# The queries' softmax denominators: one sum on VectorE in place of a tree of additions on GpSimd, and a new order on four engines

## The chip, the cores and the metric

One core of one Trainium2 chip runs the whole program in one launch. The metric is the device time of an execution in microseconds (us). The kernel before took 640.22, 637.19 and 633.03 us in three executions, a median of 637.19 us.

## What is computed

Two blocks follow each other on x, 8 sequences of 1024 tokens and 256 channels, all in fp32. The first is linear attention with 16 heads of 16 channels; the second is a feed-forward layer with ternary weights. This is the first one, cut from the reference; the change touches the softmax of q:

```python
q = x @ Wq.T + bq
k = x @ Wk.T + bk
v = x @ Wv.T + bv
q, k, v = (split(q), split(k), split(v))      # (batch, heads, tokens, 16)
q = softmax(q, axis=-1)                       # over the 16 channels of a head
k = softmax(k, axis=-2)                       # over the 1024 tokens
state = einsum('bhnd,bhne->bhde', k, v)
out = einsum('bhnd,bhde->bhne', q, state)
out = layernorm(out) * ln_g + ln_b
x = layernorm(x + out @ Wo.T + bo)            # x1, the input of the feed-forward half
```

## The kernel before

**The halves.** `attention_phase` computes x1 and stores it in a scratch tensor in DRAM; then all engines meet, and `feed_forward_phase` reads it back. The change is in the attention half alone. Its work runs batch by batch (NB = 8 sequences, 8 tiles of 128 tokens each, in two groups g of four tiles). fp32 products are made of three products of fp32r parts: a tensor named `_hi` is the rounded value, written by ScalarE, and `_lo` is what is left, a subtraction on VectorE or GpSimd.

**The loop.** Each engine has a loop over b from 0 to NB + 1 in which the steps of several batches stand in an order written out by hand. An engine runs its list strictly in order, and each step begins with waits on counting semaphores. Iteration b holds, by batch:

- b + 1: `q_product` (TensorE, into one of two PSUM banks, four pieces v), `q_maximum` and `q_centre` (VectorE), `q_exponent` (ScalarE, writes `qw`), `q_denominator` (GpSimd, writes `qsum`).
- b: `k_product` into the four banks of `ring`, `k_maximum` (VectorE: `kmx`, `kbm`, `kbias`), `k_exponent` (`ek`), `q_inverse` (VectorE, `qinv`), `q_normalise` (GpSimd: `qw` times `qinv`), transposes of `qw` and `ek` into `ring`, their parts `pt_hi`, `pt_lo`, `et_hi`, `et_lo`, and `state_sum` into `sps`. GpSimd's `tok_lo` writes `xt_lo` from ScalarE's `xt_hi` (`tok_hi`), which `state_sum` reads; its `tok_c` adds a row to xt; `chan_lo` writes `xc_lo`, which the products of q and k read.
- b - 1: `sum_low` (`xe_lo`), `state_product`, `state` (VectorE: `s_f`, `r_f`, `srow`), `state_transpose`, `transposed_high` (ScalarE, `st_hi`), `state_low`, `state_project`, `projected`, `projected_high` (`r_hi`), `projected_low` (`r_lo`), and then `attend` t = 0 to 7: a product into one of two halves of `aps`, `product_stats` (VectorE, `bnA`), `product_out` (ScalarE, copies to `z`). `attend(t)` waits until `product_out(t - 2)` has emptied its half. `out_variance` (`veA`) and GpSimd's `attention_rstd` (`rsA`, a power) follow for each group, then `residual` (VectorE, `z` and `znm`).
- b - 2: ScalarE's `squares`, GpSimd's `norm_rstd` (seven small instructions, the last writes `z`), ScalarE's `normalise`, and the store.

**Beside it.** In iterations 2 and 4 VectorE rounds a weight matrix of the feed-forward half in place (`ternary_round`, `ternary_top`, and `ternary_bottom` in 2 and 8; each is one instruction over 128x2048), and in iteration 8 TensorE computes rows from it (`ternary_rows`, after the last `attend`), which VectorE copies out (`folded_rows`: `ff_u_row`, `ff_c_row`).

**The denominators.** `q_denominator` in its form before adds halves of 16 channels with four dependent GpSimd instructions per group, through a scratch tensor `qtree`. For batch 0 they are VectorE's, one `tensor_reduce` per group ahead of the loop (line 738).

Of the kernel before, what the change touches and what calls it, by code (L numbers as in the profile page):

```python
# [75 lines left out]
def attention_phase(nc, kept, x_tok, x_chan, wq, wk, wv, wo, w1, w2, vecs_d, rows_d, ident_d, mask_d, x1_scratch):  # L76
# [14 lines left out]
    with ExitStack() as ctx:  # L91
# [23 lines left out]
        qtree = sb("qtree", [P, NG, GROUP * HEADS, D // 2])  # L115
# [77 lines left out]
        q_tree = sem("q_tree")  # L193
# [69 lines left out]
        def _(pool):  # L263
# [65 lines left out]
            def q_denominator(b, g):  # L329
                if not 1 <= b < NB:  # L330
                    return
                n = NG * (b - 1) + g
                pool.wait_ge(q_exp, NG * b + g + 1)
                v = qw[:, b % 2, g * GROUP:(g + 1) * GROUP].rearrange("p t (h d) -> p (t h) d", d=D)
                nc.gpsimd.tensor_tensor(qtree[:, g], v[:, :, 0:8], v[:, :, 8:16], ALU.add).then_inc(q_tree, 1)
                pool.wait_ge(q_tree, 3 * n + 1)
# [1260 lines left out]
```

## Time and profile before

| | |
|---|---|
| executions (us) | 640.22, 637.19, 633.03; median 637.19 |
| the profiled execution | 639.02 us; span 637.2 us; mean granted TensorE clock 0.952 |
| attention half | from the start to the first load of `ff_x` at 339.13 us |
| busy, whole span | PE 559.3 (88%), DVE 527.3 (83%), ACT 463.6 (73%), POOL 427.5 (67%) |
| largest attention lines | PE 940 `attend`, PE 957 `state_sum`, POOL 280 `tok_lo` 39.4 us |

PE is TensorE's matmuls and PEld its weight loads, DVE is VectorE, ACT ScalarE, POOL GpSimd. PEld idle in front of an instruction is the cleanest sign of a wait of TensorE, since the ends of matmuls are modelled. A wait is put down to the semaphore that came last. The chain that ended last spends the feed-forward half on PE almost wholly; of the attention half it shows next to nothing by line, so that half has to be read from its own waits.

### The profile page before, as it was taken

Reading aid. Unit: us, or ns where it says so; the run is one execution under the profiler, and the core shown is the slowest. Engines: PE = TensorE matmul, PEld = TensorE weight load, DVE = VectorE, ACT = ScalarE, POOL = GpSimd, SP = SyncE. Lnnn points to the kernel's source line nnn. Section 1 sums busy time; section 2 is a strip of 40 time slices with the busy share of each in tenths; the row PEclk is TensorE's granted clock in tenths of the full one; section 3 lists DMA queues with packets and bytes.
Section 4 is the critical chain, followed back from the end, with each engine's and each line's share of the span. In section 5 each row is a group of like instructions: output and inputs, shape, how many; then the busy total and the mean of one; then the engine's idle time right before and its main releaser. Section 6 shows DMA issues by size and latency. Waiting matters only on the chain. (4 is left out here: it accounts for less than half of the span.)

```text
span 637.2 us, 10896 instructions
## 1 busy us (share of the span) xinstructions
PE 559.3 (88%) x3584; PEld 505.6 (79%) x3584; DVE 527.3 (83%) x1309; ACT 463.6 (73%) x906; POOL 427.5 (67%) x414
## 2 busy tenths in 40 slices
PE   1879999889998989979652999999999999999991
PEld 1769989879988979968551799888888888888890
DVE  3895798997979897868443479999999999999985
ACT  1253668476865848575554788999999999999983
POOL 0277887969988887783341556766767666776661
PEclk9899999989999999989685799999999999999996
DMA  7411004070402203030105100211112222200002
GB/s 269 168 67 67 1 6 194 1 264 2 163 36 91 109 2 133 1 132 2 66 8 225 33 34 2 62 55 53 53 46 67 68 67 67 68 34 33 34 34 99
DMA packets 10712, 46.53 MB, mean 73 GB/s; under 512 B 1312, under 2 KB 1568, under 8 KB 8352
## 3 DMA queue, kind: packets, MB, share of 16 engines
q1 hardware_dynamic: 10656, 45.83, 19.9%
q8 instruction: 29, 0.48, 0.3%
q14 instruction: 27, 0.22, 0.1%
HBM read 29.02 MB, written 16.81 MB: 72 GB/s over the span
## 5 line engine op out<-in xcount | busy, mean ns | idle before, releaser
L1518 PE MATMUL yps<-ff_w,ff_a_hi 128*128 128x258 f32 x512 | 125.8, 282 | 0.0
L1518 PE MATMUL yps<-ff_w,ff_a_lo 128*128 128x258 f32 x512 | 125.7, 282 | 0.0
L1502 PE MATMUL hps<-ff_ht_hi,t 128*128 128x512 f32 x256 | 107.5, 420 | 2.6 <-DVE ff_ht_lo L1301 2.6
L1309 DVE SCALAR_TENSOR_TENSOR ff_a_lo<-hps,ff_rho,ff_a_hi 128x512 fp32r<-128x512 f32 x128 | 91.6, 742 | 15.2 <-ACT ff_a_hi L1227 14.2
L1502 PE MATMUL hps<-ff_ht_lo,t 128*128 128x512 f32 x256 | 102.8, 402 | 0.0
L1518 PEld LDWEIGHTS yps<-ff_w,ff_a_hi 128*128 128x128 f32 x512 | 96.9, 189 | 3.4
L1518 PEld LDWEIGHTS yps<-ff_w,ff_a_lo 128*128 128x128 f32 x512 | 96.7, 189 | 3.3
L1213 ACT ACTIVATE hps<-hps,bias 128x512 f32<-128x512 f32 x128 | 83.9, 670 | 17.6 <-PE hps L1502 16.2
L1185 POOL TENSOR_TENSOR ff_accp<-ff_accp,ff_sq 128x512 f32<-128x512 f32 x64 | 83.9, 1311 | 10.6 <-ACT ff_sq L1225 5.9
L1225 ACT ACTIVATE ff_sq<-hps 128x512 f32<-128x512 f32 x128 | 78.4, 612 | 0.6
L1227 ACT CAST ff_a_hi<-hps 128x512 fp32r<-128x512 f32 x128 | 77.3, 604 | 0.0
L1172 POOL TENSOR_TENSOR ff_x1c<-ff_x,ff_c_row 128x512 f32<-128x512 f32 x32 | 37.4, 1191 | 48.5 <-DVE ff_z L1370 48.5
L1502 PEld LDWEIGHTS hps<-ff_ht_hi,t 128*128 128x128 f32 x256 | 49.1, 192 | 17.9 <-DVE ff_ht_lo L1301 5.5
L940 PE MATMUL aps<-r_hi,pt_hi 128*128 128x384 f32 x128 | 48.2, 376 | 11.8 <-DVE r_lo L510 6.7
L1502 PEld LDWEIGHTS hps<-ff_ht_lo,t 128*128 128x128 f32 x256 | 49.4, 193 | 7.6
L411 ACT COPY z<-aps 128x256 f32<-128x256 f32 x64 | 23.4, 382 | 38.2 <-DVE bnA L684 38.0
L280 POOL TENSOR_TENSOR xt_lo_then_t<-xt,xt_hi 128x1024 fp32r<-128x1024 f32 x16 | 39.4, 2462 | 16.9 <-ACT xt_hi L380 16.9
L684 DVE BATCH_NORM_STATS2 bnA<-aps 128x6 f32<-128x256 f32 x64 | 26.8, 427 | 27.1 <-PE aps L940 27.0
L271 POOL TENSOR_TENSOR xc_lo<-xc,xc_hi 128x1024 fp32r<-128x1024 f32 x14 | 33.5, 2396 | 19.1 <-ACT xc_hi L373 19.1
L940 PE MATMUL aps<-r_lo,pt_hi 128*128 128x384 f32 x128 | 44.5, 347 | 0.0
L940 PE MATMUL aps<-r_hi,pt_lo 128*128 128x384 f32 x128 | 44.3, 346 | 0.0
L1370 DVE SCALAR_TENSOR_TENSOR ff_z<-ff_yc,ff_gain,ff_x1c 128x256 f32<-128x256 f32 x64 | 41.6, 691 | 0.0
(186 smaller groups left out, 1716.8 us busy)
## 6 DMA issues: line engine op xcount, KB each, us to landing
x_scratch<-z SPq DMA_DIRECT2D x16, 514.0 KB, 2.8
ff_x<-x_scratch SPq DMA_DIRECT2D x16, 514.0 KB, 4.9
xc<-in_x_chan_dram SPq DMA_DIRECT2D x8, 1024.0 KB, 6.8
xt<-in_x_tok_dram SPq DMA_DIRECT2D x8, 1024.0 KB, 4.8
out_dram<-ff_z SPq DMA_DIRECT2D x16, 512.0 KB, 3.4
w_raw<-in_w_dram SPq DMA_DIRECT2D x2, 1024.0 KB, 4.8
rows<-in_rows_dram SPq DMA_DIRECT2D x1, 512.0 KB, 4.2
w_raw<-in_wq_dram SPq DMA_DIRECT2D x1, 256.0 KB, 2.6
```

The source lines that it names most:

```text
L271: nc.gpsimd.tensor_tensor(xc_lo[:, b % 2, c], xc[:, c], xc_hi[:, b % 2, c].bitcast(F32), ALU.subtract).then_inc(xc_lo_ok, 1)
L280: nc.gpsimd.tensor_tensor(xt_lo[:, ts], xt[:, b % 2, ts], xt_hi[:, ts].bitcast(F32), ALU.subtract).then_inc(xt_lo_ok, 1)
L940: last = nc.tensor.matmul(out, l, r, start=(c == 0 and k == 0), stop=(c == CH - 1 and k == 2), skip_group_check=True)
L1172: nc.gpsimd.tensor_tensor(x1c[:, k % 2, ts], x1[:, k % XB, ts, 0:C], c_row[:].rearrange("p (o c) -> p o c", o=1).to_broadcast([P, n, C]), ...
L1185: nc.gpsimd.tensor_tensor(accp[:], a, sq[:, m], ALU.add).then_inc(sum_p, 1)
L1213: nc.scalar.activation(ring(k, m), ring(k, m), ACT.Gelu, bias=bias1[:, m:m + 1]).then_inc(gelu_ok, 1)
L1225: nc.scalar.activation(sq[:, m], ring(k, m), ACT.Square).then_inc(sq_ok, 1)
L1227: nc.scalar.copy(a_hi[:, m % DEPTH], ring(k, m)).then_inc(hi_ok, 1)
L1309: nc.vector.scalar_tensor_tensor(out=a_lo[:, m % DEPTH], in0=ring(k, m), scalar=rho[:, m:m + 1], in1=a_hi[:, m % DEPTH].bitcast(F32), op0= ...
L1370: nc.vector.scalar_tensor_tensor(out=z[:, k % 2, t], in0=yc[:, t], scalar=gain[:, t:t + 1], in1=x1c[:, k % 2, t], op0=ALU.mult, op1=ALU.ad ...
L1502: mm = nc.tensor.matmul(ring(k, m), t1[:, c, m * P:(m + 1) * P], h[:, k % 2, c], start=(c == 0 and j == 0), stop=(c == CH - 1 and j == 1))
L1518: last = nc.tensor.matmul(yps[:, t, 0:C + 2], a[:, m % DEPTH, t * P:(t + 1) * P], w2[:, m], start=(m == 0 and j == 0), stop=(m == FC - 1 a ...
```

## The change

`q_denominator` moves from GpSimd to VectorE as one `tensor_reduce` per group over the 16 channels, for every batch; `qtree` and its semaphore go. The order of the steps is written anew on GpSimd, ScalarE, VectorE and TensorE; the sync engine's list is as before, and no other instruction is added or removed. One wait changes: ScalarE's second `absolute_sums` waits for both groups of squares of its batch. Some steps of VectorE and GpSimd have moved from the end of iteration b to the start of iteration b + 1, so their argument is one less (`residual(b - 1, 0)` at an end is `residual(b - 2, 0)` at the next start).

```diff
-        qtree = sb("qtree", [P, NG, GROUP * HEADS, D // 2])
...
 # GpSimd
-            def q_denominator(b, g):
...
-                pool.wait_ge(q_exp, NG * b + g + 1)
...
-                nc.gpsimd.tensor_tensor(qtree[:, g], v[:, :, 0:8], v[:, :, 8:16], ALU.add).then_inc(q_tree, 1)
...
-                nc.gpsimd.tensor_tensor(qsum[:, g], qtree[:, g, :, 0], qtree[:, g, :, 1], ALU.add).then_inc(q_sum, 1)
...
-            for c in range(CH):
-                chan_lo(1, c)
             for b in range(NB + 2):
+                chan_lo(b + 1, 0)
+                chan_lo(b + 1, 1)
+                tok_c(b - 1, 0)
+                attention_rstd(b - 2, 0)
+                attention_rstd(b - 2, 1)
                 norm_rstd(b - 2, 0)
                 norm_rstd(b - 2, 1)
                 q_normalise(b, 0)
+                tok_lo(b, 0)
                 q_normalise(b, 1)
-                tok_lo(b, 0)
-                q_denominator(b + 1, 0)
                 tok_lo(b, 1)
-                chan_lo(b + 2, 0)
-                tok_c(b, 0)
-                tok_c(b, 1)
-                attention_rstd(b - 1, 0)
-                chan_lo(b + 2, 1)
-                attention_rstd(b - 1, 1)
-                q_denominator(b + 1, 1)
+                tok_c(b - 1, 1)
 # ScalarE
                 squares(b - 2, 1)
+                normalise(b - 2, 0)
                 transposed_high(b - 1)
-                normalise(b - 2, 0)
-                k_exponent(b, 0)
                 normalise(b - 2, 1)
                 projected_high(b - 1)
+                k_exponent(b, 0)
                 tok_hi(b)
                 q_exponent(b + 1, 0)
+                product_out(b - 1, 0)
                 chan_hi(b + 2)
-                product_out(b - 1, 0)
...
 # VectorE
+            def q_denominator(b, g):
+                if not 0 <= b < NB:
+                    return
+                dve.wait_ge(q_exp, NG * b + g + 1)
+                nc.vector.tensor_reduce(qsum[:, g], qw[:, b % 2, g * GROUP:(g + 1) * GROUP].rearrange(
+                    "p t (h d) -> p (t h) d", d=D), AX_X, ALU.add).then_inc(q_sum, 1)
...
             for b in range(NB + 2):
+                residual(b - 2, 0)
+                sum_low(b - 1)
+                residual(b - 2, 1)
+                k_maximum(b, 0)
...
                 state(b - 1)
...
-                k_maximum(b, 0)
                 q_inverse(b, 0)
...
                 q_maximum(b + 1, 2)
                 q_centre(b + 1, 2)
-                product_stats(b - 1, 0)
+                q_inverse(b, 1)
...
+                pt_low(b, 1)
+                product_stats(b - 1, 5)
+                q_denominator(b + 1, 0)
+                product_stats(b - 1, 6)
+                et_low(b, 0)
                 out_variance(b - 1, 0)
...
+                et_low(b, 2)
+                et_low(b, 3)
+                q_denominator(b + 1, 1)
                 out_variance(b - 1, 1)
                 e_inverse(b)
-                et_low(b, 2)
-                et_low(b, 3)
-                residual(b - 1, 0)
-                sum_low(b)
-                residual(b - 1, 1)
                 if b in (2, 4):
                     ternary_round(b // 2 - 1)
                     ternary_top(b // 2 - 1)
                 if b == 2:
                     ternary_bottom(0)
                 if b == NB:
                     folded_rows()
 # TensorE
                 k_product(b, 0, 0)
+                k_product(b, 0, 1)
                 state_product(b - 1)
-                k_product(b, 0, 1)
+                k_product(b, 1, 0)
                 q_product(b + 1, 0)
...
                 q_product(b + 1, 2)
+                attend(b - 1, 0)
+                q_transposes(b, 0)
                 q_product(b + 1, 3)
-                q_transposes(b, 0)
-                attend(b - 1, 0)
                 attend(b - 1, 1)
...
```

**VectorE where iteration 3 ends and 4 begins.** Rows name the line, the operation, what is written and read, and the semaphores waited for; the kernel before has

```order
L664 TENSOR_SCALAR veA<-mvA 128x4 [waits a_var]
L698 RECIPROCAL einv<-esum 128x2 [waits k_exp]
L510 TENSOR_TENSOR et_lo<-ring,et_hi 128x512 [waits et_hi_ok] x2
L673 SCALAR_TENSOR_TENSOR z,zsum<-z,rsA,xt 128x256 [waits y_out,xt_c_ok,a_rstd]
L673 SCALAR_TENSOR_TENSOR z,zsum<-z,rsA,xt 128x256 x3
L678 TENSOR_SCALAR znm<-zsum 128x4 [waits z_ok]
L510 TENSOR_TENSOR xe_lo<-sps,xe_hi 128x512 [waits xe_hi_ok]
```

and the changed one

```order
L488 TENSOR_TENSOR et_lo<-ring,et_hi 128x512 [waits et_hi_ok] x2
L536 TENSOR_REDUCE qsum<-qw 128x64 [waits q_exp]
L645 MEMSET fence 128x1 [waits a_stat]
L647 BN_AGGR mvA<-bnA 128x2 x4
L649 TENSOR_SCALAR veA<-mvA 128x4 [waits a_var]
L683 RECIPROCAL einv<-esum 128x2 [waits k_exp]
L658 SCALAR_TENSOR_TENSOR z,zsum<-z,rsA,xt 128x256 [waits y_out,xt_c_ok,a_rstd]
L658 SCALAR_TENSOR_TENSOR z,zsum<-z,rsA,xt 128x256 x3
L663 TENSOR_SCALAR znm<-zsum 128x4 [waits z_ok]
L488 TENSOR_TENSOR xe_lo<-sps,xe_hi 128x512 [waits xe_hi_ok]
```

The second group's sum and variance now stand between the last `et_lo` and the residual, ahead of `xe_lo`.

**GpSimd from the normalised queries of one iteration to the second `rsA`.** Before:

```order
L299 TENSOR_TENSOR qw<-qw,qinv 128x1024 [waits q_inv] x2
L280 TENSOR_TENSOR xt_lo_then_t<-xt,xt_hi 128x1024 [waits xe_mm,xt_hi_ok]
L335 TENSOR_TENSOR qtree<-qw 128x512 [waits q_exp]
L337 TENSOR_TENSOR qtree<-qtree 128x64x4 [waits q_tree]
L340 TENSOR_TENSOR qtree<-qtree 128x64x2 [waits q_tree]
L343 TENSOR_TENSOR qsum<-qtree 128x64 [waits q_tree]
L280 TENSOR_TENSOR xt_lo_then_t<-xt,xt_hi 128x1024 [waits xe_mm,xt_hi_ok]
L271 TENSOR_TENSOR xc_lo<-xc,xc_hi 128x1024 [waits k_mm,xc_hi_ok]
L290 TENSOR_TENSOR xt<-xt,c_row 128x1024 [waits xt_lo_ok] x2
L308 TENSOR_TENSOR rsA<-veA,nhalf 128x4 [waits a_eps]
L271 TENSOR_TENSOR xc_lo<-xc,xc_hi 128x1024 [waits k_mm,xc_hi_ok]
L308 TENSOR_TENSOR rsA<-veA,nhalf 128x4 [waits a_eps]
```

and changed

```order
L297 TENSOR_TENSOR qw<-qw,qinv 128x1024 [waits q_inv]
L278 TENSOR_TENSOR xt_lo_then_t<-xt,xt_hi 128x1024 [waits xe_mm,xt_hi_ok]
L297 TENSOR_TENSOR qw<-qw,qinv 128x1024 [waits q_inv]
L278 TENSOR_TENSOR xt_lo_then_t<-xt,xt_hi 128x1024 [waits xe_mm,xt_hi_ok]
L288 TENSOR_TENSOR xt<-xt,c_row 128x1024 [waits xt_lo_ok]
L269 TENSOR_TENSOR xc_lo<-xc,xc_hi 128x1024 [waits k_mm,xc_hi_ok] x2
L288 TENSOR_TENSOR xt<-xt,c_row 128x1024 [waits xt_lo_ok]
L306 TENSOR_TENSOR rsA<-veA,nhalf 128x4 [waits a_eps] x2
```

The tree is gone; one `qw` product now stands behind the first `xt_lo`, and both `xc_lo` stand ahead of both `rsA`.

**VectorE at the end of the attention half** (iteration 8 and what follows). Before:

```order
L664 TENSOR_SCALAR veA<-mvA 128x4 [waits a_var]
L673 SCALAR_TENSOR_TENSOR z,zsum<-z,rsA,xt 128x256 [waits y_out,xt_c_ok,a_rstd]
L673 SCALAR_TENSOR_TENSOR z,zsum<-z,rsA,xt 128x256 x3
L678 TENSOR_SCALAR znm<-zsum 128x4 [waits z_ok]
L673 SCALAR_TENSOR_TENSOR z,zsum<-z,rsA,xt 128x256 [waits y_out,xt_c_ok,a_rstd]
L673 SCALAR_TENSOR_TENSOR z,zsum<-z,rsA,xt 128x256 x3
L678 TENSOR_SCALAR znm<-zsum 128x4 [waits z_ok]
L592 COPY ff_u_row<-qps 128x256 [waits f_rows]
```

and changed

```order
L649 TENSOR_SCALAR veA<-mvA 128x4 [waits a_var]
L577 COPY ff_u_row<-qps 128x256 [waits f_rows]
L578 SCALAR_TENSOR_TENSOR ff_c_row<-qps,wstep,rows 128x256
L658 SCALAR_TENSOR_TENSOR z,zsum<-z,rsA,xt 128x256 [waits y_out,xt_c_ok,a_rstd]
L658 SCALAR_TENSOR_TENSOR z,zsum<-z,rsA,xt 128x256 x3
L663 TENSOR_SCALAR znm<-zsum 128x4 [waits z_ok]
```

The copies that wait for `f_rows` have moved ahead of the last batch's residuals.

## Rows read from the trace of the kernel before

**Rows 1.** Weight loads of the state product's first matmul, by start, duration, idle before

```profile
57.78 0.19 PEld L896 LDWEIGHTS sps<-w_hi,xe_hi 128*128 128x128 f32 x1 [0.45 <-DVE xe_lo L510]
...
92.39 0.19 PEld L896 LDWEIGHTS sps<-w_hi,xe_hi 128*128 128x128 f32 x1 [1.00 <-DVE xe_lo L510]
...
127.52 0.19 PEld L896 LDWEIGHTS sps<-w_hi,xe_hi 128*128 128x128 f32 x1 [1.39 <-DVE xe_lo L510]
...
165.25 0.19 PEld L896 LDWEIGHTS sps<-w_hi,xe_hi 128*128 128x128 f32 x1 [0.29 <-DVE xe_lo L510]
...
200.38 0.19 PEld L896 LDWEIGHTS sps<-w_hi,xe_hi 128*128 128x128 f32 x1 [1.40 <-DVE xe_lo L510]
...
236.73 0.19 PEld L896 LDWEIGHTS sps<-w_hi,xe_hi 128*128 128x128 f32 x1 [1.43 <-DVE xe_lo L510]
...
269.39 0.19 PEld L896 LDWEIGHTS sps<-w_hi,xe_hi 128*128 128x128 f32 x1 [0.44 <-DVE xe_lo L510]
```

**Rows 2.** Who waited for whom, 57 to 300 us: total us, times, longest us

```profile
PEld aps L940 <- ACT z L411: 8.6, 12, 1.5
...
PEld sps L896 <- DVE xe_lo L510: 6.4, 7, 1.4
```

**Rows 3.** VectorE's timeline in iteration 4: start, duration, what

```profile
160.91 1.30 DVE L673 SCALAR_TENSOR_TENSOR z<-z,rsA,xt 128x256 f32<-128x256 f32 x1
...
185.94 2.45 DVE L664 TENSOR_SCALAR veA<-mvA 128x4 f32<-128x4 f32 x1
...
194.18 1.29 DVE L510 TENSOR_TENSOR et_lo<-ring,et_hi 128x512 fp32r<-128x512 f32 x2 [0.49 <-ACT et_hi L437]
```

**Rows 4.** GpSimd's timeline in the same iteration

```profile
178.25 2.46 POOL L280 TENSOR_TENSOR xt_lo_then_t<-xt,xt_hi 128x1024 fp32r<-128x1024 f32 x1 [2.45 <-ACT xt_hi L380]
...
185.97 2.40 POOL L271 TENSOR_TENSOR xc_lo<-xc,xc_hi 128x1024 fp32r<-128x1024 f32 x1
```

**Rows 5.** Busy time of the instructions that touch `qtree`, in iteration 4

```profile
165.25:200.38 35.13, 6.28 (x11) 1.00 0.23 91
```

**Rows 6.** VectorE's two denominators of batch 0, ahead of the loop

```profile
30.81 2.34 DVE L738 TENSOR_REDUCE qsum<-qw 128x64 f32<-128x1024 f32 x2
```

**Rows 7.** GpSimd's groups of instructions, 100 to 300 us: busy us, mean ns, idle before

```profile
L290 POOL TENSOR_TENSOR xt<-xt,c_row 128x1024 f32<-128x1024 f32 x12 | 28.4, 2387 | 0.0
L299 POOL TENSOR_TENSOR qw<-qw,qinv 128x1024 f32<-128x1024 f32 x12 | 23.0, 1940 | 0.5 <-DVE qinv L558 0.4
...
L308 POOL TENSOR_TENSOR rsA<-veA,nhalf 128x4 f32<-128x4 f32 x12 | 13.1, 1088 | 4.8 <-DVE veA L664 4.7
```

**Rows 8.** VectorE's busy time on `w_raw` at the end of iteration 2 (fourth number)

```profile
129.33:133.16 3.83, 0.00 (x0) 0.00 (x0) 3.76 (x3) 0.00 (x0) 1.00 0.64 252
```

**Rows 9.** TensorE's weight load for `state_transpose` behind it

```profile
134.26 0.20 PEld L907 LDWEIGHTS sps<-ident,r_f 128*128 128x128 f32 x2 [2.21 <-DVE r_f L622]
```

**Rows 10.** The stretch after that: busy us by engine, then the granted clock (0.72)

```profile
134.00:140.00 6.00, 5.74 (x28) 5.16 (x29) 5.23 (x14) 5.26 (x11) 5.24 (x10) 0.72 0.96 337
```

**Rows 11.** VectorE's timeline in iteration 0

```profile
39.15 2.31 DVE L604 TENSOR_TENSOR kbm<-kmx,vecs 128x1 f32<-128x1 f32 x1
```

**Rows 12.** Timelines at the end of the attention half: ScalarE, VectorE, TensorE

```profile
306.07 0.37 ACT L417 CAST st_hi<-sps 128x256 fp32r<-128x256 f32 x1 [0.60 <-PE sps L907]
306.70 2.08 ACT L455 ACTIVATE z<-z,nmr,rsZ 128x256 f32<-128x256 f32 x4 [0.26 <-POOL z L327]
...
311.17 0.81 ACT L423 CAST r_hi<-r_f 128x768 fp32r<-128x768 f32 x1
...
308.67 0.87 DVE L644 SCALAR_TENSOR_TENSOR r_f<-u_row,nmean,sps 128x256 f32<-128x256 f32 x2 [1.74 <-PE sps L916]
...
324.69 0.48 DVE L673 SCALAR_TENSOR_TENSOR z<-z,rsA,xt 128x256 f32<-128x256 f32 x1
...
328.71 0.47 DVE L593 SCALAR_TENSOR_TENSOR ff_c_row<-qps,wstep,rows 128x256 f32<-128x256 f32 x1
...
323.50 3.84 PE L840 MATMUL qps<-xt_lo_then_t,vparts 128*128 128x256 f32 x32
```

More of the change, by code:

```diff
@@ L462, in absolute_sums @@
                     if n == 1 and h == 0:
-                        act.wait_ge(z_sq, T)
+                        act.wait_ge(z_sq, 2 * T)
                     nc.scalar.activation(f_junk, f_raw[:, h * F:(h + 1) * F], ACT.Abs,
@@ L488, in _ @@
                 product_out(b - 1, 3)
+                pt_high(b, 1)
                 product_out(b - 1, 4)
-                pt_high(b, 1)
+                et_high(b, 0)
                 product_out(b - 1, 5)
-                et_high(b, 0)
+                et_high(b, 1)
                 pt_high(b, 2)
                 pt_high(b, 3)
-                et_high(b, 1)
-                product_out(b - 1, 6)
-                product_out(b - 1, 7)
                 q_exponent(b + 1, 1)
@@ L500, in _ @@
                 et_high(b, 3)
+                product_out(b - 1, 6)
+                product_out(b - 1, 7)
                 if b in (1, 3):
@@ L736, in _ @@
             for g in range(NG):
-                dve.wait_ge(q_exp, g + 1)
-                nc.vector.tensor_reduce(qsum[:, g], qw[:, 0, g * GROUP:(g + 1) * GROUP].rearrange(
-                    "p t (h d) -> p (t h) d", d=D), AX_X, ALU.add).then_inc(q_sum, 1)
+                q_denominator(0, g)
             def folded_rows_out():
@@ L758, in _ @@
                 state_low(b - 1)
-                q_inverse(b, 1)
                 q_centre(b + 1, 0)
@@ L763, in _ @@
                 q_centre(b + 1, 1)
+                projected_low(b - 1)
                 k_maximum(b, 1)
@@ L766, in _ @@
                     folded_rows_out()
-                projected_low(b - 1)
+                product_stats(b - 1, 0)
                 q_maximum(b + 1, 2)
                 q_centre(b + 1, 2)
-                product_stats(b - 1, 0)
+                q_inverse(b, 1)
                 product_stats(b - 1, 1)
@@ L773, in _ @@
                 product_stats(b - 1, 2)
+                q_centre(b + 1, 3)
                 product_stats(b - 1, 3)
-                q_centre(b + 1, 3)
                 pt_low(b, 0)
                 product_stats(b - 1, 4)
-                out_variance(b - 1, 0)
-                product_stats(b - 1, 5)
-                pt_low(b, 1)
-                et_low(b, 0)
-                product_stats(b - 1, 6)
-                product_stats(b - 1, 7)
+                pt_low(b, 1)
[3 more added lines that the diff above has]
+                et_low(b, 0)
+                out_variance(b - 1, 0)
                 pt_low(b, 2)
@@ L786, in _ @@
                 et_low(b, 1)
+                product_stats(b - 1, 7)
+                et_low(b, 2)
+                et_low(b, 3)
+                q_denominator(b + 1, 1)
                 out_variance(b - 1, 1)
                 e_inverse(b)
-                et_low(b, 2)
-                et_low(b, 3)
-                residual(b - 1, 0)
-                sum_low(b)
-                residual(b - 1, 1)
                 if b in (2, 4):
@@ L996, in _ @@
                 q_product(b + 1, 1)
-                k_product(b, 1, 0)
                 state_project(b - 1)
@@ L1011, in _ @@
                 attend(b - 1, 5)
-                q_transposes(b, 2)
                 e_transposes(b, 0)
                 attend(b - 1, 6)
+                e_transposes(b, 1)
+                q_transposes(b, 2)
                 attend(b - 1, 7)
                 q_transposes(b, 3)
-                e_transposes(b, 1)
                 state_sum(b, 0)
```

12 lines of the change are left out of this document (removed).

## The prediction

> **What bounds the kernel now.** I read the chain of waits first: it lies in the feed-forward half, on TensorE, and the change touches nothing there, so that half keeps its time. In the attention half the order is by iterations, and the start of the state product's first weight load marks each of them [rows 1]. Iterations 1 to 6 take 34.61, 35.13, 37.73, 35.13, 36.35 and 32.66 us. Then the table of waits tells what TensorE waits for: 8.6 us for ScalarE's copy out of `aps`, 6.4 us for `xe_lo` [rows 2]. In iteration 4 the second is 1.40 us and the first about 1.7 (my estimate, 8.6 over the five iterations with that wait), so TensorE's own work is some 32.0 us (35.13 - 3.1). Iteration 6, where GpSimd and ScalarE prepare no further batch, comes within 0.7 us of that. TensorE is the floor, and an iteration that starves it costs some 3 us more.
>
> Why it starves is in two places. After the fifth product's statistics VectorE computes `veA`, a 128x4 operation, and it takes 2.45 us, from 185.94 to 188.39; GpSimd's `xc_lo` ran from 185.97 to 188.37 [rows 3, 4]. The sixth statistics, the copy and `attend(7)` queue behind it. The same happens to the first `z` of the residual (1.30 us at 160.91, 0.48 elsewhere [rows 3, 12]), and `xe_lo` is queued behind the residual.
>
> **The change, part by part.**
>
> *Trees and sums.* 14 trees of four instructions leave GpSimd. The `qtree` row of iteration 4 shows 6.28 us for 11 instructions, the two trees of one iteration and most of a third [rows 5]; taken as 6.28 x 8 / 11 that would be 4.6 us, and somewhat more since each tree's first and dearest instruction weighs in: some 5 us per iteration. GpSimd is on no path of TensorE's by itself, so I count nothing for it. VectorE gets 14 reductions of 1.15 us from start to start (2.34 for two [rows 6]). The first stands behind `product_stats(5)`: what it delays is `product_stats(6)`, and TensorE has transposes and `attend(6)` (about 1.4 us) meanwhile, so 0. The second stands ahead of the residual, in the path to `xe_lo`.
>
> *The path to `xe_lo`.* In iteration 4 the last `et_lo` ends at 195.47 [rows 3]. Add 1.15 (reduction), 0.5 (variance, inverse), 1.75 (four residuals of 0.41 from start to start and `znm`) and 0.6: `xe_lo` at 199.5. TensorE now does two pieces of `k_product` first, not one; the state product started at 200.38 after 1.40 of waiting, so one piece ended at 198.98 less the gap and the second, 1.4 us, would end at about 200.5. There is 1 us in hand: the 6.4 us of waits go, except where the ternary weights come in (below).
>
> *`veA`.* It moves behind `product_stats(6)` and `et_lo(0)`, so no copy that TensorE waits for queues behind it. But `pt_lo(2)`, `pt_lo(3)` and `et_lo(1)` do, and `e_transposes(b, 2)` waits for those. GpSimd will again be in a 2.4 us instruction at that time. I count the wait as shrunk from 1.4 to at most 0.3 per iteration, with another 0.4 left where `attend(3)` waits for a copy behind `chan_hi`. That leaves TensorE 32.0 + 0.7 = 32.7 us.
>
> *GpSimd's loop.* There is a cycle through the batches: `xt_hi`, then on GpSimd, in the new order, two `xt_lo` (2.46 each), one `qw` product (1.94), two `xt` sums (2.39 each), two `xc_lo` (2.40 each) and the first `rsA` (1.09): 17.5 us [rows 4, 7]. Before, the same stretch held one `xc_lo` and no `qw` product, but a tree. The rest of the cycle is the residual, squares, norms, `normalise`, `r_hi`, `k_exponent`, `xt_hi`: before, from 160.91 to 178.25, 17.3 us [rows 3, 4], of which I take off 0.8 (the blocked `z`), and 1.6 for a second blocked `z` and for `xe_lo` standing between: 14.9. Together 32.4, and with 0.6 for handoffs 33.0 us. This is just over TensorE's 32.7, so I take 33.0 for iterations 1, 2 and 4, and 32.7 for iteration 6, where GpSimd has no `xc_lo`. Sum: 131.7 against 137.5, **-5.8 us**.
>
> *Iterations 3 and 5.* The rounding of weights (3.76 us after iteration 2 [rows 8], 2.5 for its two instructions after iteration 4) stood behind both residuals and delayed `r_f`: TensorE waited 2.21 us [rows 9] and then ran at a granted clock of 0.72 for 6 us, between full (2.4 GHz) and half (1.2 GHz) [rows 10], some 1.7 us lost. Now it stands ahead of the residual and delays `xe_lo`: by 3.76 - 1.4 = 2.4 and by 1.1 us (1.4, TensorE's extra piece, as the cover). I assume the clock falls again after the longer wait: 33.0 + 2.4 + 1.7 = 37.1 and 34.1, against 37.73 and 36.35: **-2.9 us**.
>
> *Iteration 0.* `kbm` took 2.31 us beside GpSimd's first `xt_lo` [rows 11], and `kbias` after it was held by the tree. Now GpSimd waits there for `q_inverse(0, 1)`, which VectorE reaches later, so `kbias` is free. Between 0 and 2.4 us are to be had; nearer the upper end: **-1.6 us**.
>
> *Iteration 7.* Without pieces of q to cover it, TensorE waits for `st_hi` and `r_lo` in both orders: 0.
>
> *The end.* Two losses. ScalarE's `st_hi` (306.07) now stands behind `normalise(6, 0)`, which ends at 308.78; from `st_hi` to the end of `r_f` it took 3.47 us, so `r_hi` starts at 312.3, not 311.17: +1.1 [rows 12]. And VectorE's copies of `ff_u_row`, `ff_c_row` now stand ahead of the last residuals and wait for 32 matmuls that run from 323.50 to 327.34: the residual that began at 324.69 begins at about 328.2, +3.5, and squares, norms and the last store hang on it [rows 12]. Both add to the start of the second half, since all engines meet there: **+4.6 us**, rounded down to 4.5 for overlap of handoffs.
>
> **Sum:** -5.8 - 2.9 - 1.6 + 4.5 = -5.8 us. The profiled execution's 639.02 gives 633.2; against the median of 637.19, which I take since it stands for more executions, **631.4 us**.
>
> **A rule weighed.** A `tensor_reduce` that reads SBUF beside GpSimd at work has no row here: the two of batch 0 ran while GpSimd waited. Its bounds are 1.15 us, and 1.15 + 2.40 if it waits out a GpSimd instruction as `veA` did; I take 1.15, the row of the same instruction. The Trainium skill, "SBUF — State Buffer", section "Who interferes with whom", says that a `tensor_reduce` on trn2 never contends for the port pair that VectorE shares with GpSimd. By that rule the sum stands as it is. The page "Perfetto Trace Analysis", section "Optimizing Scalar/DVE Operations", speaks against the change: because of that shared port, moving work between these two engines might not help. By it the sum would be rival 2's.
>
> **The rivals.**
>
> 1. *The gain of the steady iterations is eaten by the cycle* (0.22). It is 33.0 us against TensorE's 32.7 with nothing in hand, and `st_hi` now waits for `normalise` besides; if it closes at 34.5, iterations 1 to 5 lose 1.5 us each and iteration 0 gives nothing: 631.4 + 7.5 + 1.6 = 640.5 us. For it: GpSimd's `rsA` comes behind 4.8 us of `xc_lo`. Against it: GpSimd sheds some 5 us.
>
> 2. *The reductions contend with GpSimd* (0.12): the second stands at a time when GpSimd is in `xc_lo` or `xt`. If each waits out an instruction, 2.40 us, there are 2.40 more in the path to `xe_lo`, with 1 in hand, and about 1 us more behind `product_stats(5)`: 2.4 us an iteration for 1 to 6, +14.4: 645.8 us, slower. It decides from 1 us of lateness on.
>
> 3. *All fits* (0.15): period 32.4 (TensorE's 32.0 and 0.4 of waits), no fall of the clock in iteration 3, iteration 0 at its best: -0.6 x 5 - 1.7 - 0.8 gives 625.9 us.
>
> 4. *The end costs nothing* (0.04), because something later than the residuals sets it: 626.9 us.
>
> My forecast has 0.47, with its own range of 628 to 636. **The range** is 625.5 to 641: it leaves out rival 2 and the outer parts of the rest. A change of this kernel under 1% (6.4 us) can't be told from none. Faster by over 1% (under 630.8): rivals 3 and 4 and 0.20 of the forecast, 0.39. Within 1%: 0.26 of the forecast and rival 1, 0.48. Slower by over 1%: 0.13.
>
> **What would show it.** The state product's first weight load without a wait in iterations 1, 4 and 6, with one of 2 us or more after iteration 2; iterations of 32.5 to 33.5 us; the reduction at 1.2 us throughout (else rival 2); `rsA` ending before VectorE is through with the last `et_lo` (else rival 1); `st_hi` behind `normalise`; the last residual beginning after `ff_c_row`, and the first `ff_x` load less early than the iterations alone would give. The prediction is wrong if iterations stay at 35 us though the waits for `xe_lo` are gone, since another step then sets the period, or if the feed-forward half changes.

## The result, and the profile after

The changed kernel is slower: 658.03 us (median of four executions, 656.84 to 659.26) against 638.71 us for the kernel before on the same chip. The ratio is 1.032, with a 95% interval of 1.028 to 1.036. The profiled execution has a span of 656.2 us against 637.2 and a granted clock of 0.94 against 0.952. GpSimd is busy for 387.7 us in place of 427.5 and VectorE for 550.1 in place of 527.3: the work moved as the change says.

The marks come first, the weight loads of the state product in the changed kernel, one per iteration (start, duration, idle before in brackets):

```profile
56.01 0.19 PEld L881 LDWEIGHTS sps<-w_hi,xe_hi 128*128 128x128 f32 x1
94.80 0.19 PEld L881 LDWEIGHTS sps<-w_hi,xe_hi 128*128 128x128 f32 x1
134.95 0.19 PEld L881 LDWEIGHTS sps<-w_hi,xe_hi 128*128 128x128 f32 x1 [0.72 <-DVE xe_lo L488]
173.16 0.19 PEld L881 LDWEIGHTS sps<-w_hi,xe_hi 128*128 128x128 f32 x1
212.06 0.19 PEld L881 LDWEIGHTS sps<-w_hi,xe_hi 128*128 128x128 f32 x1 [0.93 <-DVE xe_lo L488]
251.13 0.19 PEld L881 LDWEIGHTS sps<-w_hi,xe_hi 128*128 128x128 f32 x1
283.63 0.19 PEld L881 LDWEIGHTS sps<-w_hi,xe_hi 128*128 128x128 f32 x1
314.87 0.19 PEld L881 LDWEIGHTS sps<-w_hi,xe_hi 128*128 128x128 f32 x1 [1.61 <-DVE xe_lo L488]
```

Against [rows 1] the waits for `xe_lo` are nearly gone, as predicted, and yet iterations 1 to 5 take 38.79, 40.15, 38.21, 38.90 and 39.07 us. The table of waits from 57 to 310 us (total us, times, longest us) names what came instead, a line that [rows 2] did not have:

```profile
PEld ring L967 <- DVE pt_lo L488: 22.1, 10, 4.4
PEld sps L901 <- DVE st_lo L488: 3.9, 3, 2.5
PEld aps L925 <- ACT z L389: 3.3, 8, 1.1
PEld sps L881 <- DVE xe_lo L488: 1.7, 2, 0.9
```

L967 is `e_transposes`. VectorE's timeline in iteration 4 shows why `pt_lo` is late:

```profile
193.06 1.20 DVE L536 TENSOR_REDUCE qsum<-qw 128x64 f32<-128x1024 f32 x1
...
195.56 5.91 DVE L649 TENSOR_SCALAR veA<-mvA 128x4 f32<-128x4 f32 x1
201.39 1.28 DVE L488 TENSOR_TENSOR pt_lo<-ring,pt_hi 128x512 fp32r<-128x512 f32 x2
```

and GpSimd's timeline and TensorE's weight loads beside it:

```profile
192.09 2.38 POOL L288 TENSOR_TENSOR xt<-xt,c_row 128x1024 f32<-128x1024 f32 x1
194.43 4.72 POOL L269 TENSOR_TENSOR xc_lo<-xc,xc_hi 128x1024 fp32r<-128x1024 f32 x2
199.10 2.35 POOL L288 TENSOR_TENSOR xt<-xt,c_row 128x1024 f32<-128x1024 f32 x1
201.55 1.02 POOL L306 TENSOR_TENSOR rsA<-veA,nhalf 128x4 f32<-128x4 f32 x1
```

```profile
197.53 0.19 PEld L942 LDWEIGHTS sps<-et_lo,xt_hi 128*128 128x128 f32 x1
202.12 1.57 PEld L967 LDWEIGHTS ring<-ident,ek 128*128 128x128 f32 x8 [4.39 <-DVE pt_lo L488]
```

The 128x4 addition takes 5.91 us, where the second one of an iteration takes 0.17. It begins in the first `xc_lo` and ends when GpSimd's back-to-back run of `xc_lo`, `xc_lo`, `xt` has ended and GpSimd itself must wait (its `rsA` needs `veA`). In [rows 3, 4] the same addition ended with one `xc_lo`, after 2.45 us. In iterations 1 to 5 it takes 5.87, 5.84, 4.12 (it begins in the second `xc_lo` there), 5.91 and 5.87 us, and TensorE waits 4.36, 4.32, 2.58, 4.39 and 4.35 us. Then its clock falls between its levels of 2.4 and 1.2 GHz, as two windows show (us, busy PE, PEld, DVE, ACT, POOL, granted clock, DMA share, GB/s); nothing had run on TensorE in the first of them:

```profile
200.00:202.00 2.00, 0.00 (x0) 0.00 (x0) 2.00 (x3) 0.00 (x0) 1.90 (x2) 0.88 0.00 0
202.00:206.00 4.00, 3.88 (x22) 3.88 (x23) 3.55 (x7) 1.72 (x4) 0.57 (x1) 0.63 0.01 4
```

At the end the two things foreseen are there, ScalarE's `st_hi` behind `normalise` and VectorE's residual behind the rows (the answers to [rows 12]):

```profile
319.99 2.07 ACT L433 ACTIVATE z<-z,nmr,rsZ 128x256 f32<-128x256 f32 x4 [1.23 <-POOL z L325]
321.97 0.35 ACT L395 CAST st_hi<-sps 128x256 fp32r<-128x256 f32 x1
```

```profile
341.88 0.43 DVE L577 COPY ff_u_row<-qps 128x256 f32<-128x256 f32 x1 [2.62 <-PE qps L825]
342.22 0.47 DVE L578 SCALAR_TENSOR_TENSOR ff_c_row<-qps,wstep,rows 128x256 f32<-128x256 f32 x1
342.61 0.47 DVE L658 SCALAR_TENSOR_TENSOR z<-z,rsA,xt 128x256 f32<-128x256 f32 x1
```

### The profile page after: what moved, and what is told of

The parts are those of the page before. It is cut to its first block and busy times, and to the rows that moved or that the text cites. A ratio compares the mean times of both kernels' runs of the same rounds, so it can differ in the third digit from the quotient of the medians.

```text
span 656.2 us, 10854 instructions
## 1 busy us (share of the span) xinstructions
PE 563.7 (86%) x3584; PEld 510.3 (78%) x3584; DVE 550.1 (84%) x1323; ACT 466.0 (71%) x906; POOL 387.7 (59%) x358
## 5 line engine op out<-in xcount | busy, mean ns | idle before, releaser
L415 ACT CAST et_hi<-ring 128x512 fp32r<-128x512 f32 x32 | 18.6, 588 | 37.4 <-PE ring L967 37.4
L306 POOL TENSOR_TENSOR rsA<-veA,nhalf 128x4 f32<-128x4 f32 x16 | 19.2, 1198 | 42.8 <-DVE veA L649 42.1
```

## The experiments

The theory after the result (theory 1): GpSimd's run of instructions without a gap holds `veA`, and TensorE waits behind it. Its rival (theory 2): VectorE is simply loaded too much, by the reductions and by contention spread over many instructions.

**EPS added on GpSimd.** The changed kernel; VectorE no longer does the 128x4 addition at all.

```diff
 # GpSimd, attention_rstd
+                pool.wait_ge(a_var, T * b + GROUP * (g + 1))
+                nc.gpsimd.tensor_tensor(veA[:, gs], mvA[:, gs, 1], eps[:, gs], ALU.add).then_inc(a_eps, 1)
 # VectorE, out_variance
-                nc.vector.tensor_scalar(veA[:, gs], mvA[:, gs, 1], EPS, None, ALU.add).then_inc(a_eps, 1)
```

> The changed kernel, with the addition of EPS to the variances (`veA`, 128x4) moved from VectorE to GpSimd, just ahead of `rsA`. In the changed kernel the first `veA` of iterations 1 to 5 took 4.12 to 5.91 us and the transposes behind it waited 2.58 to 4.39 us. Theory 1 (a VectorE instruction that wants the port shared with GpSimd is held until GpSimd's whole train of `xt`, `xc_lo`, `xc_lo`, `xt` is through): nothing on VectorE asks for the port in that stretch, the waits of TensorE for `pt_lo` in iterations 1 to 5 fall under 0.5 us and the falls of its clock with them, iterations come down from 39 to 33-34.5 us, and the time from 658 to 633 us (628 to 638). Theory 2 (the two reductions per batch, 1.2 us each on a VectorE that is 84% busy, are what costs): little changes, 655 us (650 to 659).

Measured: 631.26 us, ratio to before 0.991 (0.987 to 0.994). An instruction of 0.17 us, done twice per batch, that changes its engine takes 27 us off the changed kernel, and from 57 to 310 us TensorE no longer waits for `pt_lo` at all. GpSimd's run is still there (its two `xc_lo` take 4.75 us from 183.66), and the reductions are still on VectorE. Theory 2 falls.

**The tree back on GpSimd, in the new order.** VectorE's two reductions leave the loop as well, which the lines below do not show.

```diff
                 tok_lo(b, 0)
+                q_denominator(b + 1, 0)
                 q_normalise(b, 1)
...
                 chan_lo(b + 1, 1)
+                q_denominator(b, 1)
                 tok_c(b - 1, 0)
```

> The changed kernel's order with the old way of the denominators: GpSimd's tree of four additions (group 0 behind the first `xt_lo`, group 1 between the second `xc_lo` and the `xt` sum of the next iteration), no reduction on VectorE in the loop. Theory 1 (GpSimd's train holds the port): `veA` still falls into a train of `xt`, `xc_lo`, `xc_lo` and the tree's first addition, so it is held 4 to 6 us and the time stays at 652 to 662 us. Theory 2 (the reductions cost): VectorE loses 2.3 us of work per iteration and the time falls to 642 us (638 to 646).

Measured: 668.59 us, ratio 1.049 (1.046 to 1.053), slower than either theory said. `veA` is held for 1.8 us in four of the iterations and for 7.63 in one, but another wait is longer: the residual waits for `rsA`, 23.7 us in five times, and TensorE 19.5 us for `xe_lo` behind it. VectorE at `veA` in iterations 2 and 4:

```profile
120.41 7.63 DVE L669 TENSOR_SCALAR veA<-mvA 128x4 f32<-128x4 f32 x1
...
200.16 1.84 DVE L669 TENSOR_SCALAR veA<-mvA 128x4 f32<-128x4 f32 x1
```

Both begin 0.6 us after GpSimd has begun an `xt`. In iteration 4 the addition gets in when that `xt` ends, in iteration 2 only behind the `xt`, both `xc_lo` and the tree's first addition. So one place in one program can go either way. With the tree, GpSimd is late in this order; how late it would be with EPS added there too was not run.

**The reductions alone, in the old order.**

```diff
 # GpSimd
-                q_denominator(b + 1, 0)
-                q_denominator(b + 1, 1)
 # VectorE
                 product_stats(b - 1, 5)
+                q_denominator(b + 1, 0)
...
                 et_low(b, 3)
+                q_denominator(b + 1, 1)
```

> The kernel before with the replacement alone: the trees leave GpSimd, VectorE has one `tensor_reduce` behind `product_stats(5)` and one behind the last `et_lo`; every other step in the old order. Theory 1: `veA` now meets GpSimd in `xt_lo`, `xc_lo`, `xt`, `xt` with no tree among them, and is held for up to three of them: first `veA` of an iteration 4 to 7 us in place of 2.1 to 2.5, iterations 37 to 39 us, 650 us (645 to 660). Theory 2 (only the load on VectorE counts): `veA` stays at 2.5 us or less, and the time rises by at most 1.15 us per reduction, to 645 us (640 to 652).

Measured: 652.73 us, ratio 1.020 (1.013 to 1.026), within theory 1's range, but less than 1 us outside theory 2's; the trace decides. The profiled execution was the fastest of the four (646.05 us). VectorE and then GpSimd in iteration 4:

```profile
188.89 4.20 DVE L651 TENSOR_SCALAR veA<-mvA 128x4 f32<-128x4 f32 x1
```

```profile
186.03 2.40 POOL L269 TENSOR_TENSOR xc_lo<-xc,xc_hi 128x1024 fp32r<-128x1024 f32 x1
188.39 4.67 POOL L288 TENSOR_TENSOR xt<-xt,c_row 128x1024 f32<-128x1024 f32 x2
193.17 1.02 POOL L306 TENSOR_TENSOR rsA<-veA,nhalf 128x4 f32<-128x4 f32 x1
```

The addition now meets the pair of `xt` and outlasts both; TensorE's wait for the copy out of `aps` grows from 8.6 [rows 2] to 18.7 us. Theory 2 had `veA` at 2.5 us or less, and it takes 3.8 to 4.2 us in iterations 1 to 5. Where `veA` falls in GpSimd's list matters in the old order too; the reductions were added in the same edit, so this run does not give a share of the 2% to each.

**Gaps in GpSimd's run.** The changed kernel with nothing moved; three instructions of GpSimd wait for the one ahead of them in its own queue.

```diff
 # GpSimd, chan_lo and tok_c
+                if c == 1:
+                    pool.wait_ge(xc_lo_ok, CH * b + 1)
+                elif b >= 3:
+                    pool.wait_ge(xt_c_ok, NG * (b - 2) )
...
+                if g == 0 and b + 2 < NB:
+                    pool.wait_ge(xc_lo_ok, CH * (b + 3))
```

> The changed kernel, with three waits added on GpSimd's own queue: each of `xc_lo`, `xc_lo` and the `xt` sum behind them waits for the GpSimd instruction just ahead of it to have finished. No other engine's order or work changes. Theory 1a (the port is given up when the next GpSimd instruction is not yet issued): `veA` gets in at the first such gap, takes at most 2.4 us in place of 5.9, TensorE's wait for `pt_lo` falls from 4.4 to about 1 us, and the time from 658 to 640 us (634 to 645). Theory 1b (the port goes back only when GpSimd has nothing to do): the three waits change nothing, 658 us (655 to 661). Theory 2 (load of the reductions): the same, 658 us.

Measured: 635.95 us, ratio 0.998 (0.996 to 1.001). GpSimd and VectorE in iteration 4:

```profile
182.35 2.40 POOL L273 TENSOR_TENSOR xc_lo<-xc,xc_hi 128x1024 fp32r<-128x1024 f32 x1 [0.17 <-POOL xt L294]
184.92 2.39 POOL L273 TENSOR_TENSOR xc_lo<-xc,xc_hi 128x1024 fp32r<-128x1024 f32 x1 [0.17 <-POOL xc_lo L273]
```

```profile
183.33 1.45 DVE L655 TENSOR_SCALAR veA<-mvA 128x4 f32<-128x4 f32 x1
```

`veA` gets in at the first gap of 0.17 us. GpSimd does more waiting and the kernel is 22 us faster than the changed one. This shows theory 1 directly: VectorE gets in where GpSimd's next instruction is not yet there.

**Two probes of the hold by itself.** The first:

> The whole computation is left out; this program has ten short stages and no TensorE work. In each, GpSimd runs a lead addition over 128x1024 and then a train of four more, about 2.4 us each; VectorE waits for the lead, does 0, 1 or 2 reductions of about 1.2 us (which are not held, by the runs so far), and then one tiny probe over 128x4. Stages, as train / reductions ahead / probe: 1 plain / 1 / tensor_scalar; 2 plain / 0 / tensor_scalar; 3 the train's instructions carry waits for another engine that are long satisfied / 1 / tensor_scalar; 4 each waits for the one just ahead / 1 / tensor_scalar; 5 each waits for the one two ahead / 1 / tensor_scalar; 6 plain / 1 / tensor_tensor of two SBUF inputs; 7 plain / 1 / tensor_reduce; 8 one input a row read again and again, as in the xt sums / 1 / tensor_scalar; 9 plain / 2 / tensor_scalar; 10 as 5 / 0 / tensor_scalar. Theory 1a (a held instruction gets in only when GpSimd's next instruction has not been issued): about 1.2 us in stage 4, about 8.4 in stages 1, 3, 5 and 8, and 7.2 in stage 9. Theory 1c (only some form, a satisfied wait or the broadcast row, keeps the port): the held instruction gets in after one instruction, about 1.2 us, in stage 1, and later only in stage 3, 5 or 8. Theory 2 (the load of reductions does it): nothing over 1.3 us anywhere. Stage 7, a reduction as probe: 0.2 us by what the changed kernel's reductions showed; stage 6 is open, between 0.2 and 8.4.

Measured, VectorE's probe and GpSimd's lead and train in stage 1, then the probes of stage 2, 4 and 7:

```profile
11.58 0.96 DVE L119 TENSOR_SCALAR tiny<-small 128x4 f32<-128x4 f32 x1
...
22.26 2.22 DVE L119 TENSOR_SCALAR tiny<-small 128x4 f32<-128x4 f32 x1 [2.52 <-POOL lead L143]
...
47.36 1.09 DVE L119 TENSOR_SCALAR tiny<-small 128x4 f32<-128x4 f32 x1
...
83.63 0.16 DVE L123 TENSOR_REDUCE tiny<-small 128x1 f32<-128x4 f32 x1
```

```profile
7.88 2.34 POOL L143 TENSOR_TENSOR lead<-src 128x1024 f32<-128x1024 f32 x1 [7.44 <-ACTq L81]
10.18 9.23 POOL L158 TENSOR_TENSOR dst<-src 128x1024 f32<-128x1024 f32 x4
```

The probe at 11.58 ends at 12.54, where the first of the four must end (10.18 + 9.23 / 4 = 12.49), not at 19.4. So it was in every stage with a tensor_scalar, with waits or without. The tensor_tensor with two SBUF inputs took 0.96 too, and the reduction was not held at all. (In stage 4 each instruction of the train waits for the one ahead, so there is a gap.) That is theory 1c's number for stage 1, but no form of the train kept VectorE out in the rest. Theory 1a, that a run without a gap never lets VectorE in, is too strong as it stands. The second probe looked for what the kernel adds:

> The whole computation is left out; as in the first probe GpSimd runs a lead and then a train of four instructions over 128x1024, and VectorE a reduction of 1.2 us and then a tensor_scalar over 128x4. There the probe always got in when the GpSimd instruction ended that was running (0.97 us after a reduction), even in trains without a gap, while in the changed kernel veA outlasted two or three boundaries. Ten stages ask what makes the difference: 1 plain again; 2 the train in place with a broadcast row (as the xt sums); 3 with fp32r outputs (as xc_lo); 4 two of one and two of the other; 5 the probe's input strided (as veA's); 6 four aggregations of statistics ahead of it; 7 ScalarE busy beside it; 8 TensorE busy beside it; 9 and 10 all together, with one and two reductions ahead. If one of these is the cause, its stage shows 3.3, 5.6 or 7.9 us where the others show about 1. If none is, all show about 1 to 2.3 us, and what decides at the first boundary stays open.

Measured: every stage ends at the first boundary (0.96 to 0.99 us in stages 1 to 5, 7 and 8, 0.55 and 0.58 behind the aggregations, 1.65 with two reductions ahead). None of the suspects is the cause by itself, nor are they all together in stages 9 and 10.

**EPS on GpSimd in the old order.** The same edit on the kernel before.

> The kernel before (tree on GpSimd, old order) with only the addition of EPS to veA moved from VectorE to GpSimd, ahead of the power. Theory 1: veA is held 1.5 to 2.5 us an iteration here, with the sixth statistics and attend(7) behind it; taken away, iterations 1 to 6 lose some 1 us each of the waits for the copy out of aps: 631 us (628 to 635). It would also say that the new order as such is worth little once veA is out of VectorE's queue. Theory 2 (it is the number of VectorE's instructions beside GpSimd, not this one): within 2 us of 637.

Measured: 637.54 us, ratio 1.001 (0.998 to 1.004). Theory 1's number was wrong, and theory 2's came out; the trace shows that it did so for another reason. VectorE, then GpSimd, in iteration 4:

```profile
193.08 2.62 DVE L673 SCALAR_TENSOR_TENSOR z<-z,rsA,xt 128x256 f32<-128x256 f32 x1 [0.26 <-POOL rsA L310]
```

```profile
193.02 2.39 POOL L271 TENSOR_TENSOR xc_lo<-xc,xc_hi 128x1024 fp32r<-128x1024 f32 x1
```

`veA` no longer waits, and TensorE's wait for the copy out of `aps` falls from 8.6 to 1.9 us. But the first residual now meets the whole of the second `xc_lo`: it takes 2.62 us in place of 1.30 [rows 3], and TensorE waits 14.0 us for `xe_lo` from 57 to 310 us, where it waited 8.0 before (6.4 of it in [rows 2], which end at 300). The gain of 6.7 us was given back one step later, all but 0.7 us. In the new order the residual stands behind all of GpSimd's big instructions (mean 0.48 us), and there the same edit pays.

**The end.** On the kernel with EPS on GpSimd, first the two copies moved back behind the residuals:

```diff
                 residual(b - 2, 1)
+                if b == NB + 1:
+                    folded_rows()
...
-                if b == NB:
-                    folded_rows()
```

> The changed kernel with EPS added on GpSimd (as in the run that took 631.3 us), and the two copies of ff_u_row and ff_c_row moved back behind the last batch's residuals. My term for the end: these copies wait for 32 matmuls and delay the last residual by 3.5 us, so 631.3 - 3.5 = 627.8 us (626 to 629.5), and the end (last state product to the first ff_x load) falls from 42.2 to 38.7. Rival: the end is set by something else that is as late (the store of the last batch, TensorE's rows themselves): within 1 us of 631.3.

Measured: 627.28 us, ratio 0.987 (0.982 to 0.992). From the last state product to the first load of `ff_x` it takes 39.0 us in place of 42.2: 3.2 of the 3.5 forecast. Then `st_hi` as well:

```diff
+                if b == NB:
+                    transposed_high(b - 1)
                 normalise(b - 2, 0)
-                transposed_high(b - 1)
+                if b != NB:
+                    transposed_high(b - 1)
```

> As the run before it, and in iteration 8 alone ScalarE's st_hi stands ahead of normalise(6, 0) again. My term for that: 1.1 us more, so 626.7 us (625 to 628.5), about 1.7% under the kernel before, and an end of 37.6. Rival: TensorE's wait for st_hi is covered by what comes later (the residual waits for GpSimd or VectorE), and the run equals the one before within 0.5 us.

Measured: 627.54 us, ratio 0.985 (0.980 to 0.990). The end takes 38.2 us in the trace, 0.8 less, against 1.1 forecast; the executions do not tell the two kernels apart, so by them the rival stands as well.

**The store that came too late.** The last trace shows a wait that the kernel before did not have. The sync engine's DMA starts, ScalarE's copy into `z`, TensorE's weight load and a window behind it, all in iteration 3:

```profile
126.40 0.33 SPq L237 DMA_DIRECT2D xt<-in_x_tok_dram  x1
126.78 1.18 SPq L257 DMA_DIRECT2D w_raw<-in_w_dram  x1
128.00 0.43 SPq L231 DMA_DIRECT2D xc<-in_x_chan_dram  x1
131.14 2.88 SPq L244 DMA_DIRECT2D x_scratch<-z  x2
```

```profile
141.88 0.37 ACT L391 COPY z<-aps 128x256 f32<-128x256 f32 x1 [3.35 <-DMA x_scratch<-z]
```

```profile
142.31 0.19 PEld L928 LDWEIGHTS aps<-r_hi,pt_hi 128*128 128x128 f32 x1 [2.41 <-ACT z L391]
```

```profile
144.00:148.00 4.00, 3.62 (x13) 3.52 (x14) 1.80 (x4) 3.08 (x8) 4.00 (x3) 0.58 0.00 0
```

The store of batch 1 is issued behind 3 MB of loads; the copy of the next batch's product into `z` must wait for it. The changed kernel has it too (1.92 us there), and so has the run with the copies behind the residuals (1.92 us). The edit issues the weights' load behind the store:

```diff
                 store(b - 2)
+                if b == 3:
+                    sp.wait_ge(f_tern, 1)
+                    sp.dma_start(f_raw, w2.rearrange("p a f -> p (a f)")).then_inc(f_in, 16)
                 tok_load(b + 1)
...
-                if b == 2:
-                    sp.wait_ge(f_tern, 1)
-                    sp.dma_start(f_raw, w2.rearrange("p a f -> p (a f)")).then_inc(f_in, 16)
```

> The kernel of the last run (EPS on GpSimd, both repairs of the end; 627.5 us, 0.985 of before) with one transfer issued later: the second feed-forward weight matrix, 1 MB, is loaded in iteration 3 behind the store of batch 1, not in iteration 2 ahead of it. In the last run's trace ScalarE's first copy into z in iteration 3 waited 3.35 us for that store, issued at 131.14 behind three loads of 1 MB each; the copy ran at 141.88, TensorE waited 2.41 and 1.08 us behind it, and its clock then read 0.58 over 4 us. Theory: the new order reaches that copy earlier than the old one did, and this store is the next wait. Then the waits of 3.5 us go and about 1.7 us of slow clock with them: 622.4 us (620 to 625), 0.977 of before, the stretch between the second and third marks after batch 0 at 33.5 in place of 38.4. Rival: the load of xc, which stays ahead of the store, is enough to hold it, or the weights now come too late for their absolute sums: 627 us or more.

Measured: 624.58 us (623.64 to 625.89), ratio 0.984 (0.981 to 0.987): inside the range forecast in us, but the ratio forecast was 0.977. The kernel before took 634.90 us beside it, against 637.14 beside the last run. The marks of iterations 3 and 4:

```profile
122.86 0.19 PEld L884 LDWEIGHTS sps<-w_hi,xe_hi 128*128 128x128 f32 x1 [2.38 <-DVE xe_lo L493]
...
156.45 0.19 PEld L884 LDWEIGHTS sps<-w_hi,xe_hi 128*128 128x128 f32 x1
```

Iteration 3 takes 33.6 us in place of 38.4, as forecast, and its clock stays at 1.00. The executions do not show the gain: the ratio to the kernel before fell from 0.985 to 0.984 only, and the intervals overlap. Part of the 4.9 us can be chance of one execution: in the run with only the copies moved, where the same steps stand in the same order, iteration 3 took 36.2 us: the store held ScalarE for 1.92 us, not 3.35. What is shown is that the wait is gone.

## Why the prediction was wrong

All terms, as span against the 637.2 us of before. The third column is the changed kernel with EPS on GpSimd, where the step that failed is taken out:

| term | forecast | changed kernel | with EPS on GpSimd |
|---|---|---|---|
| iterations 1, 2, 4, 6 | -5.8 | +12.8 | -3.1 |
| iterations 3, 5 | -2.9 | +3.2 | -2.9 |
| iteration 0 | -1.6 | -1.8 | -1.2 |
| iteration 7 | 0 | -1.0 | -3.0 |
| the end | +4.5 | +4.6 | +4.7 |
| feed-forward half | 0 | +1.1 | +0.4 |
| sum | -5.8 | +19.0 | -5.1 |

**The step that failed is the one on `veA`.** It said: "GpSimd will again be in a 2.4 us instruction at that time. I count the wait as shrunk from 1.4 to at most 0.3 per iteration". GpSimd was busy there as said, but the price was wrong: the addition took 5.9 us, and TensorE waited 4.3 to 4.4 us for `pt_lo` behind it in iterations 1, 2, 4 and 5 and 2.6 us in iteration 3. I had the two facts that should have made this a rival. [rows 4] showed that a GpSimd instruction holds the addition for all of its length, and the new order puts `xc_lo`, `xc_lo` and `xt` in a row just there. The bound of 0.3 was taken from a wait of 1.4 and from what I took for cover, without asking how long GpSimd stays busy without a gap. The prediction's own sign came with it: the waits for `xe_lo` are gone and another step sets a period of 38.2 to 40.2 us. A time more than 1% slower had a chance of 0.13, nearly all of it by rival 2.

Without that one instruction on VectorE all other terms together come to -5.1 us, against -5.8 forecast. That close, it is partly luck: iterations 1 to 6 gave 2.7 us less than forecast, and iterations 0 and 7 together 2.6 us more. Iterations 1, 2, 4 and 5 are 5.2 to 5.9 us longer in the second column's kernel than in the third's: 4.3 to 4.4 us is the wait, and the slower clock behind it (0.63 over 4 us in iteration 4, that is 1.5 us) is about the rest. In iteration 3 the two are level (38.2 and 38.0): with EPS on GpSimd the wait of 2.6 us for `pt_lo` is gone, but TensorE's waits behind the store are 1.0 us longer and its clock reads 0.59 over the 4 us after them, where it stays at 1.00 in the changed kernel.

**The path to `xe_lo`** was right. The waits for it are 1.7 us in all in place of 6.4, both after the weights' rounding (0.72 and 0.93 us; with EPS on GpSimd 2.4 and 1.3, where 2.4 and 1.1 were forecast).

**Iterations 3 and 5** came out at the forecast in the table with EPS on GpSimd, but by luck. A mark stands behind the wait for `xe_lo`, so the waits of 2.4 and 1.3 us lie in iterations 2 and 4 by the marks (34.9 and 33.7 us, and 32.5 without them, where 33.0 was forecast); the prediction booked them in 3 and 5. Without them it had 34.7 and 33.0 us for 3 and 5, and these took 38.0 and 33.2. The 3.3 us in iteration 3 are the store behind the weights' load, which I had not seen, though I had counted the sync engine's list as unchanged: ScalarE waited 2.95 us for it, TensorE 2.00 and 1.07 us behind that, and then its clock read 0.59 over 4 us. The list is unchanged: the copy that waits for its store had moved ahead. The fall of the clock that I put behind the wait for `xe_lo` did not come in this run (1.00 from 124 to 132 us). It came in the run with the copies moved, after the same wait of 2.38 us:

```profile
124.00:128.00 4.00, 3.73 (x17) 3.34 (x18) 3.90 (x15) 3.66 (x16) 1.86 (x6) 0.65 0.23 49
```

**The end** was right: +4.6 for +4.5, and in its two parts, 3.2 of 3.5 and 0.8 of 1.1, by the two runs that repair it. **Iteration 0** came out near the forecast (-1.8 and -1.2 for -1.6) with two things uncounted. Its mechanism was right: `kbm` and `kbias` take 1.34 and 0.16 us in place of 2.31 and 1.19, 2.0 us less. But the mark stands one piece of `k_product`, about 1.4 us, later in the new order, and in the changed kernel the `kmx` ahead of `kbm` already begins 0.9 us earlier (36.99 us for 37.91). Iteration 7 was counted at 0 and gave 1.0 to 3.0 us; up to 1.4 of it is no gain, since iteration 8 has no `k_product` and its mark does not move. In the changed kernel `veA` is held there too, for 2.93 us.

**The rivals.** Rival 1 is false: with EPS on GpSimd, iterations 1, 4 and 6 take 32.9, 33.7 and 32.9 us, so GpSimd's cycle does not reach 34.5 (iteration 2 takes 34.9, with 2.4 of waiting for `xe_lo` behind the rounding of weights). Rival 2 named the right resource and the wrong instruction. The reductions took 1.205 us on average beside GpSimd at work, where I took 1.15 from start to start and its price was 3.55:

```profile
L649 DVE TENSOR_SCALAR veA<-mvA 128x4 f32<-128x4 f32 x14 | 33.0, 2357 | 0.5
L658 DVE SCALAR_TENSOR_TENSOR z<-z,rsA,xt 128x256 f32<-128x256 f32 x56 | 23.9, 483 | 0.0
L536 DVE TENSOR_REDUCE qsum<-qw 128x64 f32<-128x1024 f32 x12 | 14.5, 1205 | 0.0
```

These are groups of VectorE from 57 to 330 us in the changed kernel (busy us, mean ns). 14 additions of four numbers took more than twice as long as 12 reductions of 1024, and the first line, not the new one, leads to where the 3% went. The rule of the Trainium skill that I weighed ("SBUF — State Buffer", section "Who interferes with whom": a `tensor_reduce` on trn2 does not contend) agrees with 1.205 us and with the probe's 0.16.

**What stays open.** The runs show that a gap on GpSimd lets VectorE in (1.45 us with gaps, 5.9 without), and the probes that a boundary without a gap can do so too, 18 times of 18. In the kernels it goes both ways: before, `veA` got in between `xc_lo` and `xt` five times (in three of them it had begun in the last 0.1 us of the `xt_lo` before it); after, between the same two it did not, nor between two `xt` in the run with the reductions in the old order, and in the run with the tree it went both ways at one place. In the probes the form of GpSimd's instructions, satisfied waits, the strided input, the aggregations and the other engines' load did not keep it out, singly or together. Transfers are not it either: in the changed kernel the DMA share is 0.00 or 0.01 around the `veA` of iterations 1 to 5. What decides is not known.

## What to carry to other kernels

A short VectorE instruction that GpSimd's work can hold (here a tensor_scalar or tensor_tensor on SBUF, not a tensor_reduce) can cost as much as GpSimd's whole run without a gap, not one instruction of it, and whatever is queued behind it waits as long: look in the order for three or four long instructions in a row, and for the small ones that will fall beside them. Such a small instruction can be done by the engine that holds it up, where that engine needs the result anyway. When steps move forward in one engine's list, look again at every list that stayed as it was, the transfers above all: what they delivered in time for the old order can be late for the new one.

## What the hardware showed that I had not expected

- A 128x4 addition on VectorE took up to 5.91 us beside 128x1024 instructions of 2.4 us on GpSimd, and 7.63 us in one iteration of the run with the tree. The Trainium skill, "SBUF — State Buffer", section "Who interferes with whom", says that whoever issues first has the shared port pair for the whole instruction. The probes agree (0.96 us, to the end of the instruction under way); the kernel's trace exceeds it by two instructions, and the measurement decides.
- Three added waits, with gaps of 0.17 us, made the changed kernel 22 us faster.
- The length of a wait of TensorE did not alone tell what its granted clock did. The wait of 2.38 us for `xe_lo` left it at 1.00 in the run with the weights after the store, and brought 0.65 over the next 4 us at the same place in the run with the copies behind the residuals. In the changed kernel one of 2.58 us left it at 1.00, and those of 4.36, 4.32 and 4.39 us brought 0.57, 0.50 and 0.63 over the next 4 us.
